# Q, K, V and outputs through memory in whole rows one way, a new order around score block 3, and the V turns on ScalarE

## The reference

```python
qkv = jnp.einsum('bnm,fm->bnf', x, Wqkv).reshape(b, n, N_HEADS, -1)
q, k, v = (qkv[..., :dh], qkv[..., dh:2 * dh], qkv[..., 2 * dh:])      # dh = 16
scores = jnp.einsum('bnhd,bngd->bnhg', q, k) / SCALE
attn = jax.nn.softmax(scores, axis=-1)                                 # over 16 heads
out = jnp.einsum('bnhg,bngd->bnhd', attn, v).reshape(b, n, -1)
return jnp.einsum('bni,mi->bnm', out, Wproj) + bproj
```

## Time and profile before

| | |
|---|---|
| median of 3 runs | 1350.3 us |
| the profiled execution, its own time | 1349.4 us |
| its span, first to last instruction | 1347.6 us |
| granted TensorE clock, mean | 0.891 of full speed |
| TensorE busy (products) | 1167.3 us, 87% |
| TensorE weight loads | 748.0 us, 56% |
| VectorE busy | 937.1 us, 70% |
| ScalarE busy | 722.6 us, 54% |
| GpSimd busy | 571.8 us, 42% |
| DMA | 90.64 MB in 94009 packets, 83144 of them under 2 KB |

### The profile page before, as it was taken

How to read it: one execution, slowest core, us unless ns; L and a number is a source line. 1 busy time by engine, 2 the same in 40 slices (tenths; PEclk the granted TensorE clock), 3 DMA queues, 4 the chain that set the end, 5 groups by cost and what they waited for, 6 DMA issues and landing times.

```text
span 1347.6 us, 31178 instructions
## 1 busy us (share of the span) xinstructions
PE 1167.3 (87%) x12264; PEld 748.0 (56%) x12264; DVE 937.1 (70%) x2124; ACT 722.6 (54%) x1145; POOL 571.8 (42%) x882
## 2 busy tenths in 40 slices
PE   6688899998989999998999989898999988897464
PEld 4444466655665546655566556655566555654452
DVE  3544578677775868767775778668686777755866
ACT  3223375347753575547853477545754477544653
POOL 2235435335354355245354355354462352551124
PEclk8689898799979998799988999799987998799557
DMA  5000092203902075201902056021932029026430
GB/s 188 16 1 16 18 166 23 80 9 101 127 2 79 17 167 54 66 15 68 168 2 80 9 115 113 17 64 33 174 31 64 1 87 133 2 64 114 75 96 32
DMA packets 94009, 90.64 MB, mean 67 GB/s; under 512 B 7110, under 2 KB 83144, under 8 KB 93608
## 3 DMA queue, kind: packets, MB, share of 16 engines
q1 hardware_dynamic: 82008, 77.24, 29.3%
q0 software_dynamic: 2064, 6.69, 1.6%
q10 hardware_dynamic: 9792, 4.72, 1.4%
HBM read 46.68 MB, written 41.94 MB: 66 GB/s over the span
## 4 chain that ended last, share of the span: by engine, by line
PE 57%; DVE 18%; DMA 7%; issue 6%; ACT 5%; POOL 4%; ACTq 1%; SPq 1%; DVEq 0%; POOLq 0%
PE bank L1994 54%; DVE keys L1640 2%; DVE stats L1384 2%; DMA bt<-scratch_o 2%; DVE x L1525 2%; DVE gelu L1642 2%; POOL rs L655 2%; DMA scratch_o<-stage 2%; PE bank L2004 1%; ACT x L996 1%; DVE ct L1353 1%; DMA keys<-scratch_qkv 1%; ACTq L966 1%; ACT part L873 1%; DVE x L1708 1%
## 5 line engine op out<-in xcount | busy, mean ns | idle before, releaser
L1994 PE MATMUL bank<-we,at 128*128 128x512 f16 x1536 | 373.7, 403 | 1.9 <-DVE x L1525 1.9
L1994 PEld LDWEIGHTS bank<-we,at 128*128 128x128 f16 x1536 | 154.4, 102 | 194.6 <-issue 41.6
L670 POOL TENSOR_TENSOR part<-part 128x512 f32<-128x512 f32 x64 | 84.2, 1316 | 276.5 <-ACTq L1022 276.5
L873 ACT ACTIVATE part<-bank,wexp 128x256 f32<-128x256 f32 x256 | 104.3, 470 | 159.6 <-PE bank L1994 102.9
L1525 DVE SCALAR_TENSOR_TENSOR x<-bank,wexp,x 128x256 f32<-128x256 f32 x256 | 122.7, 479 | 53.0 <-PE bank L1994 46.5
L1994 PE MATMUL bank<-bt,wqkv 128*128 128x512 f16 x576 | 137.3, 380 | 20.8 <-DVE stage L1353 12.3
L996 ACT ACTIVATE x<-x,nm,rs 128x256 f32<-128x256 f32 x184 | 100.3, 593 | 69.3 <-POOL nm L658 68.1
L1353 DVE TENSOR_TENSOR stage<-bank,stage 128x512 f16<-128x512 f32 x110 | 74.4, 686 | 82.5 <-ACT stage L873 82.2
L651 POOL TENSOR_SCALAR nm<-mv 128x2 f32<-128x2 f32 x128 | 33.4, 261 | 207.1 <-DVE mv L1389 201.5
L1994 PE MATMUL bank<-keys,blockdiag 128*128 128x16 f16 x3072 | 97.5, 193 | 21.8 <-DVE blockdiag L1554 10.0
L1994 PEld LDWEIGHTS bank<-keys,blockdiag 128*128 128x128 f16 x3072 | 96.1, 103 | 26.4 <-issue 14.5
(11 more groups left out here) (212 smaller groups left out, 2275.4 us busy)
## 6 DMA issues: line engine op xcount, KB each, us to landing
scratch_qkv<-stage SPq DMA_DIRECT2D x39, 512.0 KB, 3.3
ct<-scratch_qkv SPq DMA_DIRECT2D x112, 128.0 KB, 6.5
x_in<-in_x_dram SPq DMA_DIRECT2D x32, 256.0 KB, 2.7
bt<-scratch_o SPq DMA_DIRECT2D x16, 512.0 KB, 4.1
keys<-scratch_qkv SPq DMA_DIRECT2D x61, 128.0 KB, 6.0
out_dram<-x POOLq DMA_DIRECT2D x24, 256.0 KB, 2.7
scratch_qkv<-part SPq DMA_DIRECT2D x8, 512.0 KB, 7.8
scratch_o<-stage SPq DMA_DIRECT2D x32, 128.0 KB, 3.5
```

The costliest lines, as they stand in the source:

```text
L670: pool.tensor_tensor(part[:, 0:2, :], part[:, 0:2, :], part[:, 2:4, :], ALU.add)\
L873: return act.activation(dst, src, ACT.Copy, scale=scale)
L1994: ins = pe.matmul(dst, lhs, rhs, start=(n == 0), stop=(n == len(terms) - 1))
```

## The change

**Layout in memory.** `scratch_o` becomes a plain [256, 2048] array. A block of 128 features is stored as `by_feature`: each feature's 4 KB go in 8 pieces of 512 bytes, one per tile r, and the load takes whole rows of 4 KB over all 128 partitions. For the outputs it is the other way round: whole rows are stored and `by_feature` is read. Rows of `wqkv_t` and `wproj_t` are permuted on the host to suit. Q, K and V are two loads each instead of eight; the outputs are two stores and two loads, all from SyncE, each load waiting for its own store.

**Issuers.** ScalarE's `b_storeo` and `b_loadq` and GpSimd's `b_loadk` are gone, with the semaphore `k_rest`. In the last batch, SyncE's first Q load stands ahead of the store of block 2, the second behind it, and K's blocks are loaded in the order 3, 2.

**Turns of V.** GpSimd's `b_turnv` is gone; ScalarE's list has `b_turnv(c, 0)` ahead of exp 0 and `b_turnv(c, 1)` behind exp 1, in full turns and closing.

**Order.** `a_moe(b, 3)` on TensorE is split: bank 0 ahead of S3, banks 1 and 2 behind it, bank 3 between PT2 and PT3. On ScalarE PT2 comes ahead of `a_ln2n(0)`, O0 and O1 ahead of `a_moe(3)`, and one spread of half 1 (r = 6) goes to VectorE, also in the ending. On VectorE PT2 comes ahead of half 1's first two spreads.

```diff
+        def half_of(home, ft):
+            return home[:, 2 * C * (ft % 2):2 * C * (ft % 2 + 1)]
...
+        def by_feature(memory):
+            return memory.rearrange("a m -> (a m)").rearrange("(r p n) -> p r n", r=T, p=P)
+        def qkv_block(ft):
+            return scratch_qkv[P * ft:P * (ft + 1)]
...
-                sp.dma_start(scratch_qkv[P * ft:P * (ft + 1)], slots[s]).then_inc(stored[s], 16)
+                sp.dma_start(by_feature(qkv_block(ft)), slots[s].rearrange("p (r n) -> p r n", r=T)).then_inc(stored[s], 16)
...
+            def load_block(b, ft, home, loaded):
+                sp.wait_ge(*f_stored(b, ft))
+                sp.sem_inc(waits_held, 1)
+                sp.dma_start(half_of(home, ft), qkv_block(ft)).then_inc(loaded, 16)
             def b_loadq(b):
+                if 0 < b < NB - 1:
+                    sp.wait_ge(ff_full, 4 * b)
                 for ft in (0, 1):
-                    sp.wait_ge(*f_stored(b, ft))
-                    sp.sem_inc(waits_held, 1)
-                if b == NB - 1:
...
-                for r in range(T):
-                    sp.dma_start(home_rows(q_home(b), r), q_src[:, :, r, :].rearrange("h d n -> d h n")).then_inc(q_loaded, 16)
+                    load_block(b, ft, q_home(b), q_loaded)
             def b_loads(b):
-                for ft in (0, 1, 3, 2):
+                for ft in (0, 1, 3):
                     b_flast(b, ft)
-                b_loadq(b)
+                load_block(b, 0, q_home(b), q_loaded)
+                b_flast(b, 2)
+                load_block(b, 1, q_home(b), q_loaded)
                 b_loadk(b)
-                sp.wait_ge(k_loaded, 16 * (T * b + K_SP))
-                sp.sem_inc(waits_held, 1)
-                sp.wait_ge(k_rest, 16 * (T - K_SP))
+                sp.wait_ge(k_loaded, 32 * (b + 1))
...
-                for r in range(K_SP if b == NB - 1 else T):
-                    sp.dma_start(keys[DH * r:DH * (r + 1), :, :],
-                                 k_src[:, :, r, :].rearrange("h d n -> d h n")).then_inc(k_loaded, 16)
+                for ft in ((3, 2) if b == NB - 1 else (2, 3)):
+                    load_block(b, ft, beats_keys, k_loaded)
...
-                for r in range(T):
-                    sp.dma_start(home_rows(v_home(b), r), v_src[:, :, r, :]).then_inc(v_loaded, 16)
+                for ft in (4, 5):
+                    load_block(b, ft, v_home(b), v_loaded)
...
-                for r in range(T // 2):
-                    sp.dma_start(*o_store(r)).then_inc(o_stored, 16)
-                sp.wait_ge(o_stored, 128 * (b + 1))
-                sp.sem_inc(waits_held, 1)
                 for ht in range(KD):
-                    sp.dma_start(bt[:, ht, :, :].rearrange("p l n -> p (l n)"),
-                                 scratch_o[8 * ht:8 * ht + 8].rearrange("h d r n -> (h d) (r n)"))\
-                        .then_inc(o_loaded, 16)
+                    sp.dma_start(scratch_o[P * ht:P * (ht + 1)], ohl[:, 8 * ht:8 * ht + 8, :, :].rearrange("p h l n -> p (h l n)"))\
+                        .then_inc(o_stored[ht], 16)
+                for ht in range(KD):
+                    sp.wait_ge(o_stored[ht], 16 * (b + 1))
+                    sp.sem_inc(waits_held, 1)
+                    sp.dma_start(bt[:, ht, :, :].rearrange("p l n -> p (l n)").rearrange("p (r n) -> p r n", r=T),
+                                 by_feature(scratch_o[P * ht:P * (ht + 1)])).then_inc(o_loaded, 16)
@@ gpsimd
...
-                    if c is not None:
-                        b_turnv(c, 0)
                     a_sum(b, 1)
                 if c is not None:
                     b_s(c, 0)
                     b_s(c, 1)
-                    b_turnv(c, 1)
...
@@ scalar, turn (closing alike)
                 if c is not None:
+                    b_turnv(c, 0)
                     b_s(c, 0)
                     b_s(c, 1)
+                    b_turnv(c, 1)
...
                     b_spreadv(c, 0, range(6, T))
+                    b_pt(c, 2)
                 if b is not None:
                     a_ln2n(b, 0)
                 if c is not None:
-                    b_pt(c, 2)
                     b_pt(c, 3)
-                    b_spreadv(c, 1, range(6, T))
-                if b is not None:
-                    a_moe(b, 3)
-                if c is not None:
+                    b_spreadv(c, 1, range(7, T))
                     b_o(c, 0)
                     b_o(c, 1)
+                if b is not None:
+                    a_moe(b, 3)
+                if c is not None:
                     b_o(c, 2)
                     b_o(c, 3)
...
-                if c is not None:
-                    b_storeo(c)
@@ vector, heads
                 b_spreadv(c, 0, range(2, 5), last=True)
+                b_pt(c, 2)
                 b_spreadv(c, 1, range(0, 2))
-                b_pt(c, 2)
                 b_pt(c, 3)
-                b_spreadv(c, 1, range(2, 6), last=True)
+                b_spreadv(c, 1, range(2, 7), last=True)
@@ tensor, turn (closing alike)
                     b_pt(c, 1)
+                if b is not None:
+                    a_moe(b, 3, (0,))
+                if c is not None:
                     b_s(c, 3)
                 if b is not None:
-                    a_moe(b, 3)
+                    a_moe(b, 3, (1, 2))
                 if c is not None:
                     b_pt(c, 2)
+                if b is not None:
+                    a_moe(b, 3, (3,))
+                if c is not None:
                     b_pt(c, 3)
```

More of the change, by code:

```diff
@@ L222, in build_two_layer_postln @@
         o_hi = sem("o_hi")
-        o_stored = sem("o_stored")
+        o_stored = [sem(f"o_stored{ht}") for ht in range(KD)]
         o_loaded = sem("o_loaded")
@@ L543, in b_loadk @@
             def b_loadk(b):
-                for ft in (2, 3):
-                    sp.wait_ge(*f_stored(b, ft))
-                    sp.sem_inc(waits_held, 1)
                 if b == NB - 1:
@@ L619, in _ @@
                 sp.wait_ge(*f_stored(NB - 1, ft))
-            sp.wait_ge(o_stored, 16 * T * NB)
+            for s in o_stored:
+                sp.wait_ge(s, 16 * NB)
             for s in out_stored:
@@ L700, in b_copy @@
                     .then_inc(x3_copied, 1)
[L702 to L716, removed]
             def b_s(b, q):
@@ L959, in b_o @@
                 copy(o_part(q, HI), o_psum(q)).then_inc(o_hi, 1)
[L961 to L966, removed]
             def b_spreadv(b, hf, rs):
@@ L1052, in b_spreadq @@
                     ins.then_inc(q_spread[1], 1)
[L1054 to L1059, removed]
             def b_gelu(b, p):
@@ L1082, in b_turnv @@
             def b_turnv(b, hf):
-                act.wait_ge(v_loaded, 16 * T * (b + 1))
+                act.wait_ge(v_loaded, 32 * (b + 1))
                 copy(v_rows[hf].rearrange("p (s c) h -> p s c h", c=8),
@@ L1117, in turn @@
                 if c is not None:
-                    b_pt(c, 2)
                     b_pt(c, 3)
-                    b_spreadv(c, 1, range(6, T))
+                    b_spreadv(c, 1, range(7, T))
+                    b_o(c, 0)
+                    b_o(c, 1)
                 if b is not None:
@@ L1263, in closing @@
                 b_spreadv(c, 0, range(6, T))
+                b_pt(c, 2)
                 a_ln2n(b, 0)
-                b_pt(c, 2)
                 b_pt(c, 3)
-                b_spreadv(c, 1, range(6, T))
+                b_spreadv(c, 1, range(7, T))
+                b_o(c, 0)
+                b_o(c, 1)
                 a_moe(b, 3)
-                for q in range(4):
-                    b_o(c, q)
-                b_storeo(c)
+                b_o(c, 2)
+                b_o(c, 3)
                 a_moe(b, 4)
@@ L1317, in ending @@
                 b_pt(b, 3)
-                b_spreadv(b, 1, range(6, T))
+                b_spreadv(b, 1, range(7, T))
                 for q in range(4):
                     b_o(b, q)
-                b_storeo(b)
                 for p in range(TP):
@@ L1563, in b_turnq @@
             def b_turnq(b, hf):
-                dve.wait_ge(q_loaded, 16 * T * (b + 1))
+                dve.wait_ge(q_loaded, 32 * (b + 1))
                 if b == NB - 1:
@@ L2150, in b_s @@
                 if q == 0:
-                    pe.wait_ge(k_loaded, 16 * (T * b + (K_SP if b == NB - 1 else T)))
-                    if b == NB - 1:
-                        pe.wait_ge(k_rest, 16 * (T - K_SP))
+                    pe.wait_ge(k_loaded, 32 * (b + 1))
                 pe.wait_ge(q_spread[q // 2], (1 + q // 2) * (b + 1))
@@ L2473 @@
     wqkv = a["L1_attn_Wqkv"].reshape(HEADS, 3, DH, D).transpose(1, 0, 2, 3).reshape(3 * D, D)
+    by_dim = _np.arange(D).reshape(2, 8, DH).transpose(0, 2, 1).reshape(-1)
+    by_head = _np.arange(D).reshape(HEADS, 2, 8).transpose(1, 0, 2).reshape(-1)
+    wqkv = wqkv[_np.concatenate([by_dim, D + by_dim, 2 * D + by_head])]
     eye = _np.eye(128, dtype=_np.float32)
@@ L2489 @@
         ("wqkv_t", wqkv.T),
-        ("wproj_t", a["L1_attn_Wproj"].T),
```

(1 more changed line is left out.)

35 lines of the change are left out of this document (5 added, 30 removed).

## The result

The changed kernel takes 1333.7 us (median of 4 runs, 1331.6 to 1335.9) against 1349.2 for the kernel before in the same call (4 runs, 1346.6 to 1350.3): ratio 0.9898, 95% interval 0.9878 to 0.9919. That is 15.5 us less, where 20.3 were forecast. Its profiled execution took 1334.4 us, span 1332.6.

What follows compares the result with a forecast made beforehand. TensorE, busy 87% of the span, was taken as the bound, with its waits to cut. Order 11.0, projection waits 2.7 and ending 6.6 sum to 20.3 us, from 1349.4 to 1329.1, stated as 1329; range 1321 to 1343.

Steps and rivals of the forecast that it cites:

- Order, 11.0: Reordering around S3 shortens S3 to O2 to 17.2 us: 0.5 less in two stages, 2.0 in five, 11.0 us.
- a_moe(3, 0) takes 1.3 us and fills the idle, and S3 starts at 847.95, as before: Steady turn, TensorE: the first a_moe(3) bank fits the 1.13 us idle ahead of S3, without delaying it.
- given back: Rival, chance 0.20: VectorE's chain or TensorE's low clock takes the order's gain, leaving 9.3 us saved, 1340.
- Projection waits, 2.7: Faster output round trip, 9.6 us instead of 11.9, frees TensorE's waits ahead of the projection in steady turns: 2.7 us.
- 250 GB/s for the pieces: Assumed rate of 512-byte pieces over all 128 partitions, 2.1 us per transfer; bounds 120 and 400 GB/s.
- The slower rival: Chance 0.07: 512-byte pieces stay slow wherever they lie; output loads at 120 GB/s lengthen the trip to 14.2 us, 1360.
- Ending, 6.6: Last batch, uncovered: Q turn -3.9, V wait -1.8, order +0.9, output trip -1.8, in sum -6.6 us.
- V turns, 0: Moving steady-turn V turns from GpSimd to ScalarE: delays are covered and idle GpSimd gains nothing, worth 0.
- the bound was 5: If ScalarE's V turn 1 is not covered, its 0.7 us transpose-copy delay shows in 7 stages: 5 us.
- Q, K and V loads are covered: Steady turns: faster Q, K and V loads save nothing, since their consumers are busy or start later; worth 0.
- Parts 1 and 2: The memory layout with whole rows one way and 512-byte pieces the other, and the V turns' move to ScalarE, priced separately.

Runs made afterwards that it cites:

- memory_held: Kernel before with the new memory layout, V turns on GpSimd held until the Q spreads are done, old order: 1330.6 us, 0.9887 of before.
- after_again: The changed kernel itself, run again beside later follow-ups: 1331.8 us, 0.9881 of before.
- gpsimd_held: Changed kernel with V turns back on GpSimd, plus one wait until both engines' Q spreads are done: 1332.2 us, 0.9896 of before.
- turns_gpsimd: Changed kernel with the V turns back on GpSimd, without an added wait: 1354.3 us, 1.0050 of before.
- memory_only: Changed kernel with the order undone and V turns back on GpSimd, leaving only the new layout: 1352.3 us, 1.0029 of before.
- turns_alone: Kernel before with only its V turns moved to ScalarE: 1355.8 us, 1.0054 of before.
- no_order_2: Changed kernel with the new order and the moved spread undone, second timing: 1329.7 us, 0.9872 of before.

## Why the prediction was right or wrong

The time fell inside the range, and in good part by luck: the sum behind it was not right. Its largest term, 11.0 of 20.3 for the order, is worth nothing that the times show. The layout had 10.2 of the sum (2.7, and 7.5 of the ending without its order), and saved 15.6 alone once GpSimd's turns were held (memory_held, 1346.2 to 1330.6). In one trace of each kernel, before and memory_held, S2 to O2 gives 4.4 us, for which the sum had no term; O2 to the projection gives 5.8, where 2.7 were forecast; and from the closing's projection to the ending's it is 104.3 us instead of 112.4, 8.1 where 7.5 were forecast. No run parts the layout of Q, K and V from that of the outputs. (By its own words the sum leads to 1330.0 from the median of 1350.3, not to 1329.)

- **Order, 11.0.** Its mechanics behind S3 held: S3 to O2 at 16.9 (forecast 17.2), VectorE last. The step that failed: "a_moe(3, 0) takes 1.3 us and fills the idle, and S3 starts at 847.95, as before". In three of seven stages the bank takes 2.65 to 2.77 us at the low clock, and S3 behind it starts 1.4 to 1.7 us late; in three more transpose 1 is late, by the V turn on ScalarE. S2 to S3 grew by 6.6 in sum, so that of 13.0 gained behind S3 6.4 were left, and in after_again, with five stages at the low clock, 4.2. And most of the long stages were no longer there to be mended: with the layout in, the old order has two of them instead of five, and S2 to O2 is 159.4 in sum. In the timed comparison the order gave nothing (1331.8 with it, 1329.7 without). The rival "given back" had the outcome right for the order, and the clock as the cause in part; it looked for it in a_moe(4) or the projection, and it happened ahead of S3. Its 1340 was wrong because it left only 9.3 to the rest.
- **Projection waits, 2.7.** The waits went from 11.0 in 5 places to 6.0 in one, so steady turns lost theirs. The distance from O2 to the projection fell by more, 131.8 to 126.0 in sum in memory_held, part of it (84.7 to 82.5) ahead of a_moe(4).
- **Layout.** I took 250 GB/s for the pieces. The two loads of the ending move 243 and 255 GB/s in the windows 1282 to 1284 and 1284 to 1286, and the trip of two stores and two loads is 9.1 us where 9.6 was forecast. The slower rival, pieces at 120 GB/s anywhere, is out.
- **Ending, 6.6.** Its mechanisms were right, its size somewhat too small: Q is turned 0.6 us behind the start of the last copy (4.66 before), V's wait is gone, the trip is 2.3 shorter (forecast 1.8). From the closing's projection to the ending's it saved 7.9 us (112.4 to 104.5) where 6.6 were forecast. Behind the trip the profiled run gave 2.8 back: from the projection to the end 45.6 us instead of 42.8, by the router's clock (last section); in the second run of the same kernel it is 41.1.
- **V turns, 0.** Against a GpSimd whose turns are held, the number is right as far as the times show. Exp 0 is 0.5 us late in the turn shown, not 0.3 (VectorE waits 1.18 us for it instead of 0.70), and the late transpose 1 costs 1.9 us in sum ahead of S3, where the bound was 5; gpsimd_held, without either, takes 1332.2. But the 0 was taken against the wrong alternative. "Q, K and V loads are covered" and "Worth 0" asked only whether V is late enough to hurt and not what a V that is early sets off. Left on GpSimd, the turn runs beside VectorE's Q spreads: some 21 us between turns_gpsimd and gpsimd_held. Parts 1 and 2 had to be priced together; apart they are +4 to +5 (memory_only) and +7 to +9 (turns_alone), and my sum gave them -10.2 and 0.
- The kernel before had shown the sign of it, in order of time:
```profile
821.92 7.35 DVE L1554 TENSOR_SCALAR blockdiag<-prob,const 128x2048 f16<-128x2048 f16 x8
829.20 2.73 DVE L1554 TENSOR_SCALAR blockdiag<-shared,const 128x2048 f16<-128x2048 f16 x4
...
822.01 1.79 POOL L670 TENSOR_TENSOR part<-part 128x512 f32<-128x512 f32 x1 [5.97 <-ACTq L1022]
```
  Eight Q spreads, the first of them beside GpSimd's sums, take 7.35 us, 0.92 each, and the next four, without GpSimd, 2.73, 0.68 each: a difference by neighbour that I did not read.

What stays open: why the clock's low stretch begins where it does in each kernel, and so how much of memory_held's 4.4 us in S2 to O2 comes from the layout and how much is luck; and what the rest of its gain from O2 to the projection is, beyond the waits.

## What to carry to other kernels

A slow transfer can be what keeps two engines apart. Before speeding one up, list what starts when it lands, and what runs on the neighbouring engine at the new time; then price the transfer and its consumer as one part. A filler placed ahead of an instruction that others wait for must fit the idle time at the slower clock too, or go behind it.

## What the runs showed of the hardware

Executions of one kernel differ, and in some kernels the longer ones have the lower mean granted clock: no_order_2 took 1328.5 at 0.901 and 1337.5 at 0.893, gpsimd_held 1329.8 at 0.902 and 1339.4 at 0.893. The mean does not tell it all: the changed kernel took 1331.6 at 0.896 and 1335.9 at 0.898. It also matters which products the low stretch meets. In the profiled run of the changed kernel the twelve router products of the ending ran at half clock (granted clock 0.50 from 1304 to 1308):
```profile
1304.81 5.33 PE L1948 MATMUL bank<-ct,wrt 128*128 128x512 f16 x12
```
and in the second one of the same kernel at full (1.00 from 1304 to 1308):
```profile
1304.12 1.46 PE L1948 MATMUL bank<-ct,wrt 128*128 128x512 f16 x6
1305.78 1.46 PE L1948 MATMUL bank<-ct,wrt 128*128 128x512 f16 x6 [0.21 <-DVE ct L1307]
```
The two spans are 1332.6 and 1329.8. Effects of 2 to 3 us in this kernel can therefore not be read from one trace, and the stage sums above are no more exact than that. GpSimd's own operations stretch in the same way as VectorE's: its sum of 512 columns takes 1.79 us beside the Q spreads of gpsimd_held and 1.27 elsewhere.
